# Transposes of adjacent columns, new order lists, and the first x in two loads

## The reference

```
memory_proj = ctx @ W_mem.T
attn        = softmax(x @ memory_proj.T / sqrt(256))
mem         = attn @ memory_proj
gate        = sigmoid(concat[x, mem] @ W_gate.T + b_gate)
x1          = rmsnorm(x + gate * mem) * norm_w

q           = layernorm(x1) * g + b, @ Wq / 8          # 16 heads of 64
k, v        = split(ctx @ Wkv)
out         = softmax(q k.T, masked) v @ Wo
x2          = x1 + tanh(attn_gate) * out
y           = x2 + tanh(ff_gate) * gelu(layernorm(x2) @ W1) @ W2
```

## Time and profile before

| | |
|---|---|
| median of 3 runs | 211.98 us (211.62 to 212.43) |
| profiled execution | 211.99 us |
| its span in the trace | 210.2 us |
| TensorE matmuls | 203.1 us, 97% of the span |
| TensorE weight loads | 170.2 us, 81% |
| VectorE | 152.5 us, 73% |
| ScalarE | 130.7 us, 62% |
| GpSimd | 73.0 us, 35% |

### The profile page before, as it was taken

How to read it: one execution, slowest core, us unless ns; L and a number is a source line. 1 busy time by engine, 2 the same in 40 slices (tenths; PEclk the granted TensorE clock), 3 DMA queues, 4 the chain that set the end, 5 groups by cost and what they waited for, 6 DMA issues and landing times.

```text
span 210.2 us, 4475 instructions
## 1 busy us (share of the span) xinstructions
PE 203.1 (97%) x1497; PEld 170.2 (81%) x1497; DVE 152.5 (73%) x534; ACT 130.7 (62%) x412; POOL 73.0 (35%) x69
## 2 busy tenths in 40 slices
PE   7899999999999999999999999989999999999993
PEld 3568768988778988888878988877877799988993
DVE  2499997869987788889778889999787464234410
ACT  3378687169974696583687677768997740158400
POOL 1010427633357033145333544794385006000000
PEclk9999999999999999999999999999999999999999
DMA  6996500140000000000000000006000000100011
GB/s 192 310 371 204 174 25 2 28 176 0 3 0 2 0 5 0 3 3 0 3 0 5 0 2 3 0 0 203 3 0 3 0 0 28 53 25 0 6 50 58
DMA packets 8797, 10.19 MB, mean 48 GB/s; under 512 B 1088, under 2 KB 7872, under 8 KB 8512
## 3 DMA queue, kind: packets, MB, share of 16 engines
q1 hardware_dynamic: 8096, 9.44, 13.9%
q10 hardware_dynamic: 672, 0.39, 0.6%
HBM read 8.79 MB, written 1.05 MB: 47 GB/s over the span
## 4 chain that ended last, share of the span: by engine, by line
PE 68%; DVE 9%; issue 8%; POOL 8%; DMA 4%; SPq 2%; ACT 0%; POOLq 0%; DVEq 0%
PE bank L509 44%; PE bank L1321 5%; PE bank L1293 5%; PE bank L1433 5%; DMA probs<-in_L_xattn_W_gate_dram 4%; PE bank L1331 4%; POOL probs L623 3%; SPq L556 2%; PE bank L1276 2%; DVE xhat L1033 1%; PE bank L1359 1%; DVE expd L971 1%; POOL xhat L660 1%; DVE fused L1006 1%; POOL roots L635 1%
## 5 line engine op out<-in xcount | busy, mean ns | idle before, releaser
L623 POOL TENSOR_TENSOR probs<-expd,row_rcp 128x512 f32<-128x512 f32 x39 | 41.6, 1088 | 61.3 <-DVE row_rcp L981 61.3
L751 ACT ACTIVATE expd<-expd,neg_max 128x128 f32<-128x128 f32 x128 | 49.6, 393 | 1.5 <-DVE neg_max L971 1.4
L971 DVE CUSTOM_DVE_ANT_0 expd<-bank,mask_bias 128x128 f32<-128x128 f32 x128 | 28.5, 285 | 4.5 <-PE bank L1293 3.9
L509 PE MATMUL bank<-xhT_pair,wq_pair 128*128 128x256 f32 x192 | 26.2, 290 | 0.4 <-DVE fused L1006 0.2
L509 PE MATMUL bank<-wo_pair,oT_pair 128*128 128x256 f32 x192 | 26.2, 288 | 0.0
L509 PEld LDWEIGHTS bank<-xhT_pair,wq_pair 128*128 128x128 f32 x192 | 23.9, 190 | 2.3 <-issue 1.0
L509 PEld LDWEIGHTS bank<-wo_pair,oT_pair 128*128 128x128 f32 x192 | 24.1, 191 | 1.6 <-issue 1.0
L751 ACT ACTIVATION_READ_ACCUMULATOR expd<-expd,neg_max 128x1 f32 x128 | 24.5, 192 | 0.0
L509 PE MATMUL bank<-wq_pair,gelu_pair 128*128 128x256 f32 x192 | 23.7, 284 | 0.1
L509 PEld LDWEIGHTS bank<-wq_pair,gelu_pair 128*128 128x128 f32 x192 | 23.3, 192 | 0.4 <-DVE x_sb L1154 0.3
L1321 PE MATMUL bank<-ident,probs 128*128 128x128 f32 x160 | 21.1, 275 | 0.0
(11 more groups left out here) (155 smaller groups left out, 361.6 us busy)
## 6 DMA issues: line engine op xcount, KB each, us to landing
stage<-in_L_xattn_W_dram SPq DMA_DIRECT2D x2, 1024.0 KB, 5.2
x_sb<-in_x_dram SPq DMA_DIRECT2D x4, 256.0 KB, 7.8
wkv_sb<-in_L_xattn_Wkv_dram SPq DMA_DIRECT2D x2, 512.0 KB, 5.6
stage<-in_L_xattn_Wq_dram SPq DMA_DIRECT2D x1, 1024.0 KB, 9.5
stage<-in_L_xattn_Wo_dram SPq DMA_DIRECT2D x1, 1024.0 KB, 5.5
out_dram<-x_sb SPq DMA_DIRECT2D x8, 128.0 KB, 1.9
ctx_sb<-in_ctx_dram SPq DMA_DIRECT2D x4, 192.0 KB, 6.4
probs<-in_L_xattn_W_gate_dram SPq DMA_DIRECT2D x1, 512.0 KB, 8.3
```

The source lines that it names most:

```text
L509: last = nc.tensor.matmul(bank_ap, lhs(a), rhs(c), start=start and n == 0, stop=stop and n == 2)
L623: nc.gpsimd.tensor_tensor(probs[:, r, :].rearrange("p (h k) -> p h k", h=hb), expd[:, r, :].rearrange("p (h k) -> p h k", h=hb), row_rcp[: ...
L751: last = nc.scalar.activation(here, here, ACT.Exp, bias=neg_max[:, r, h:h + 1], scale=-1.0, accum_out=row_sum[:, r, h:h + 1])
L971: last = nc.vector.tensor_tensor_reduce(expd[:, r, h * w:(h + 1) * w], SC[n % 2][:, h * w:(h + 1) * w], mask_bias[:, first:first + w], -1. ...
```

## The change

Part k now holds the adjacent columns 128k to 128k + 127: all transposes of x, gate weights and normalised rows read neighbouring columns, and the loads of `wq`, `w1`, W_mem and the two vectors of the first layer norm are laid out to match, as `(k p)`. x of batch 0 comes as two loads of 128 rows, one behind the other on SP's queue, each with its own semaphore, and its transposes go tile by tile instead of part by part. The warm-up has six matmuls instead of eight, and they read 128 columns four times over, so that only these are zeroed. All four lists are new; they hold the same stages. Lists are cut below; hunks that only repeat a shown edit are left out.

```diff
--- before.py
+++ after.py
@@ -30,7 +30,7 @@
 FAR = 3.0e38
 RMS_EPS = 1e-6
 LN_EPS = 1e-5
-WARM_UP = 8
+WARM_UP = 6
 DUMMIES = (3, 2)
@@ -42,111 +42,110 @@
 TENSOR_ORDER = (
-    ("xT", 0), ("ctxT", 0), ("tiles",), ("y", 0), ("look", "PE"), ("branch", "PE"), ("dummy", 0), ("ctxT", "hot"),
-    ("scores", "ctx", 0, 0), ("dummy", 1), ("v", "hot", 0, 0), ("v", "hot", 0, 1), ("weights",),
-    ("spread", "ctx", 0, 0), ("xT", 1), ("ctxT", 1), ("gatemem",), ("u", 0), ("k", "hot", 0), ("k", "hot", 1),
-    ("gate", 0), ("k", "hot", 2), ("k", "hot", 3), ("k", "hot", 4), ("y", 1), ("v", "hot", 1, 0),
-    ("scores", "ctx", 1, 0), ("k", "hot", 5), ("k", "hot", 6), ("v", "hot", 1, 1), ("xhT", 0), ("v", "hot", 2, 0),
-    ("xT", 2), ("k", "hot", 7), ("ctxT", 2), ("spread", "ctx", 1, 0), ("q", 0, 0), ("q", 0, 1), ("ctxT", 3),
-    ("scores", "head", 0, 0), ("u", 1), ("q", 0, 2), ("scores", "head", 0, 1), ("gate", 1),
-    ("scores", "head", 0, 2), ("q", 0, 3), ("spread", "head", 0, 0), ("v", "hot", 2, 1), ("scores", "head", 0, 3),
-    ("av", 0, 0), ("y", 2), ("v", "hot", 3, 0), ("spread", "head", 0, 1), ("xT", 3), ("scores", "ctx", 2, 0),
-    ("wo", 0, 0), ("xhT", 1), ("y", 3), ("av", 0, 1), ("spread", "head", 0, 2), ("q", 1, 0), ("q", 1, 1),
-    ("av", 0, 2), ("scores", "head", 1, 0), ("spread", "head", 0, 3), ("q", 1, 2), ("spread", "ctx", 2, 0),
...
-    ("spread", "head", 2, 1), ("q", 3, 0), ("q", 3, 1), ("spread", "head", 2, 2), ("av", 2, 1),
-    ("scores", "head", 3, 0), ("wo", 2, 0), ("q", 3, 2), ("scores", "head", 3, 1), ("av", 2, 2), ("q", 3, 3),
-    ("h2T", 0, 0), ("spread", "head", 2, 3), ("wo", 2, 1), ("scores", "head", 3, 2), ("av", 2, 3),
...
+    ("xT", 0), ("ctxT", 0), ("tiles",), ("y", 0), ("dummy", 0), ("ctxT", "hot"), ("scores", "ctx", 0, 0),
+    ("look", "PE"), ("branch", "PE"), ("v", "hot", 0, 0), ("dummy", 1), ("v", "hot", 0, 1), ("ctxT", 1),
+    ("spread", "ctx", 0, 0), ("weights",), ("u", 0), ("gatemem",), ("ctxT", 2), ("xT", 1), ("gate", 0),
+    ("k", "hot", 0), ("k", "hot", 1), ("y", 1), ("v", "hot", 1, 0), ("k", "hot", 2), ("scores", "ctx", 1, 0),
+    ("k", "hot", 3), ("k", "hot", 4), ("v", "hot", 1, 1), ("k", "hot", 5), ("xhT", 0), ("v", "hot", 2, 0),
+    ("k", "hot", 6), ("spread", "ctx", 1, 0), ("k", "hot", 7), ("xT", 2), ("v", "hot", 2, 1), ("q", 0, 0), ("u", 1),
+    ("scores", "head", 0, 0), ("q", 0, 1), ("q", 0, 2), ("scores", "head", 0, 1), ("gate", 1),
+    ("scores", "head", 0, 2), ("y", 2), ("q", 0, 3), ("spread", "head", 0, 0), ("scores", "head", 0, 3),
+    ("av", 0, 0), ("spread", "head", 0, 1), ("v", "hot", 3, 0), ("ctxT", 3), ("scores", "ctx", 2, 0), ("xhT", 1),
+    ("wo", 0, 0), ("av", 0, 1), ("spread", "head", 0, 2), ("q", 1, 0), ("q", 1, 1), ("scores", "head", 1, 0),
...
+    ("q", 2, 3), ("spread", "head", 2, 1), ("xhT", 3), ("wo", 1, 3), ("av", 2, 0), ("scores", "head", 2, 3),
+    ("q", 3, 0), ("q", 3, 1), ("spread", "head", 2, 2), ("av", 2, 1), ("scores", "head", 3, 0), ("q", 3, 2),
+    ("wo", 2, 0), ("q", 3, 3), ("spread", "head", 2, 3), ("scores", "head", 3, 1), ("av", 2, 2), ("wo", 2, 1),
+    ("scores", "head", 3, 2), ("av", 2, 3), ("spread", "head", 3, 0), ("wo", 2, 2), ("h2T", 0, 0), ("h2T", 0, 1),
...
 )
...
 SCALAR_ORDER = (
-    ("v", "hot", 0, 0), ("weights",), ("splitk",), ("spread", "ctx", 0, 0), ("xT", 1), ("splitq", 0), ("gatemem",),
-    ("u", 0), ("splitq", 1), ("k", "hot", 0), ("splitv",), ("gate", 0), ("k", "hot", 1), ("k", "hot", 2),
-    ("fuse", 0), ("k", "hot", 3), ("k", "hot", 4), ("y", 1), ("mask",), ("rms", 0), ("rms", 1), ("rms", 2),
...
     ("wmem",), ("xT", 0), ("xpair",), ("y", 0), ("branch", "ACT"), ("hotpair",), ("exp", "ctx", 0, 0),
+    ("v", "hot", 0, 0), ("splitk",), ("spread", "ctx", 0, 0), ("weights",), ("u", 0), ("gatemem",), ("splitq", 0),
+    ("xT", 1), ("splitv",), ("gate", 0), ("k", "hot", 0), ("fuse", 0), ("y", 1), ("mask",), ("v", "hot", 0, 1),
...
 )
...
 VECTOR_ORDER = (
-    ("wmem",), ("any",), ("xT", 0), ("ctxT", 0), ("flag",), ("branch", "DVE"), ("ctxT", "hot"), ("xpair",),
-    ("scores", "ctx", 0, 0), ("hotpair",), ("norm", "ctx", 0, 0), ("v", "hot", 0, 0), ("v", "hot", 0, 1),
-    ("weights",), ("spread", "ctx", 0, 0), ("splitk",), ("xT", 1), ("ctxT", 1), ("gatemem",), ("u", 0),
...
-    ("q", 3, 0), ("q", 3, 1), ("ln2", 1), ("av", 2, 1), ("scores", "head", 3, 0), ("norm", "head", 2, 3),
-    ("spread", "head", 2, 2), ("split1", 0), ("q", 3, 2), ("scores", "head", 3, 1), ("norm", "head", 3, 0),
-    ("q", 3, 3), ("x2hat", 1), ("av", 2, 2), ("norm", "head", 3, 1), ("spread", "head", 2, 3), ("split1", 1),
...
+    ("any",), ("xT", 0), ("wmem",), ("ctxT", 0), ("flag",), ("xpair",), ("branch", "DVE"), ("ctxT", "hot"),
+    ("scores", "ctx", 0, 0), ("norm", "ctx", 0, 0), ("v", "hot", 0, 0), ("v", "hot", 0, 1), ("ctxT", 1),
+    ("spread", "ctx", 0, 0), ("hotpair",), ("weights",), ("splitk",), ("u", 0), ("gatemem",), ("ctxT", 2),
...
+    ("q", 3, 0), ("ln2", 1), ("split1", 0), ("spread", "head", 2, 2), ("norm", "head", 2, 3), ("q", 3, 1),
+    ("av", 2, 1), ("scores", "head", 3, 0), ("split1", 1), ("q", 3, 2), ("spread", "head", 2, 3),
+    ("norm", "head", 3, 0), ("scores", "head", 3, 1), ("av", 2, 2), ("x2hat", 1), ("norm", "head", 3, 1),
...
 )
...
 POOL_ORDER = (
-    ("norm", "ctx", 0, 0), ("branch", "POOL"), ("splitv",), ("rms", 0), ("norm", "ctx", 1, 0), ("xhat", 0),
-    ("splito", 0), ("splito", 1), ("norm", "head", 0, 0), ("norm", "head", 0, 1), ("rms", 1),
...
+    ("norm", "ctx", 0, 0), ("branch", "POOL"), ("splitv",), ("rms", 0), ("norm", "ctx", 1, 0), ("splito", 0),
+    ("xhat", 0), ("norm", "head", 0, 0), ("splito", 1), ("norm", "head", 0, 1), ("rms", 1), ("xhat", 1),
...
 )
@@ -375,6 +374,7 @@
         x_in = [sem(f"x_in{b}") for b in range(B)]
+        x0_rest_in = sem("x0_rest_in")
         ctx_arrived = [sem("ctx_first_in"), sem("ctx_hot_in"), sem("ctx_rest_in")]
         w_in = {n: sem(f"{n}_in") for n in ("mask", "tiles", "wmem", "wgate", "bgate", "normw", "ln", "lnq", "gates", "wkey",
                                             "wvalue", "wq", "wo", "w1", "w2")}
@@ -532,7 +532,7 @@
         def mem_view(part):
-            return gate_mem_pair[:, part, D:2 * D].rearrange("e (p k) -> e k p", k=K)
+            return gate_mem_pair[:, part, D:2 * D].rearrange("e (k p) -> e k p", k=K)
         def mem_bank(bank_ap):
             return bank_ap[:, 0:D].rearrange("e (k p) -> e k p", k=K)
@@ -558,7 +558,8 @@
             def load_x(b):
                 load(x_sb[:, b * T:(b + 1) * T, :], x[b].rearrange("(t p) d -> p t d", p=P), x_in[b])
-            load_x(0)
+            load(x_sb[:, 0, :], x[0, 0:P, :], x_in[0])
+            load(x_sb[:, 1, :], x[0, P:N, :], x0_rest_in)
             load(mask_tiles[:, :], mask.rearrange("b (t n) -> (b t) n", n=P), w_in["tiles"])
             load(wkv_sb[:, INNER:2 * INNER], wkv[:, INNER:2 * INNER], w_in["wvalue"])
             load(ctx_tiles[:, 1:B, HOT, :], ctx_in[1:B, HOT * P:M, :].rearrange("b p e -> p b e"), ctx_arrived[1])
@@ -569,10 +570,11 @@
             load(wgate_sb, w_gate.rearrange("(k p) f -> p k f", p=P), w_in["wgate"])
             load_x(1)
             load(bgate_sb[:, :], b_gate.rearrange("(a d) -> a d", a=1).to_broadcast([P, D]), w_in["bgate"])
-            load(stage[:, :].rearrange("p (k n) -> p k n", k=K), wq.rearrange("(p k) n -> p k n", k=K), w_in["wq"])
+            load(stage[:, :].rearrange("p (k n) -> p k n", k=K), wq.rearrange("(k p) n -> p k n", k=K), w_in["wq"])
             load(normw_sb[:, :], norm_w.rearrange("(a d) -> a d", a=1).to_broadcast([P, D]), w_in["normw"])
-            for i, v in enumerate((lnq_g, lnq_b)):
-                load(lnq_cols[:, i, :], v.rearrange("(p k) -> p k", k=K), w_in["lnq"])
+            with nc.allow_non_contiguous_dma(reason="two values a row"):
+                for i, v in enumerate((lnq_g, lnq_b)):
+                    load(lnq_cols[:, i, :], v.rearrange("(k p) -> p k", k=K), w_in["lnq"])
             load(mask_u8[:, :], mask.rearrange("(a b) m -> a (b m)", a=1).to_broadcast([P, B * M]),
                  w_in["mask"])
             with nc.allow_non_contiguous_dma(reason="single values"):
@@ -588,7 +590,7 @@
             load(stage[:, :].rearrange("p (i n) -> p i n", n=D), wo.rearrange("(i p) n -> p i n", p=P), w_in["wo"])
             sp.wait_ge(act["wsplit"], 4)
             sp.wait_ge(pool["wsplit"], 2)
-            load(stage[:, :].rearrange("p (k n) -> p k n", k=K), w1.rearrange("(p k) n -> p k n", k=K), w_in["w1"])
+            load(stage[:, :].rearrange("p (k n) -> p k n", k=K), w1.rearrange("(k p) n -> p k n", k=K), w_in["w1"])
             sp.wait_ge(act["wsplit"], 6)
             sp.wait_ge(dve["wsplit"], 4)
             load(stage[:, :].rearrange("p (i n) -> p i n", n=D), w2.rearrange("(i p) n -> p i n", p=P), w_in["w2"])
@@ -683,7 +685,7 @@
         @block.scalar
         def _(sc):
-            sc.dma_start(wmem_sb[:, :, :], w_mem.rearrange("(p k) e -> p k e", k=K)).then_inc(w_in["wmem"], 16)
```

(27 more changed lines are left out.)

97 lines of the change are left out of this document (49 added, 48 removed), and 35 rows, old and new, of tables (SCALAR_ORDER, TENSOR_ORDER, VECTOR_ORDER).

## The result

| | before | after |
|---|---|---|
| median | 211.75 us (211.26 to 212.43, 18 runs) | 213.6 us (211.58 to 214.75, 18 runs) |
| ratio, 95% interval | | 1.0072, 1.0052 to 1.0092 |
| span of the profiled execution | 210.2 us | 212.4 us |

The changed kernel is slower by about 1.5 us at the middle of the interval; the forecast was 1.3 us faster.

The account below looks back on a forecast made before the run. TensorE's queue was taken as the bound, matmuls busy 203.1 us, 97% of the span. Start -0.1, transposes -0.5 and lists -0.7 summed to -1.3, from 211.98 to 210.7 us; range 209.4 to 212.5.

Parts of the forecast that it names:

- The lists behind 35 us: New engine orders after 35 us: 0.7 us gained, no work added; bounds from 1.2 lost to 1.6 recovered.
- the cover of `av 2 3` and of the second `xhT`: Work hiding two old waits: 5.0 us instead of 2.7 at the first, gaining 0.7; 2.3 less at the second, even.
- The gain of the lists: Behind 35 us, the new lists give back 0.7 us at the context product that had waited 0.8.
- The transposes: Adjacent columns make 52 transposes 10 ns faster each, 110 ns start to start: 0.5 us gained on TensorE.
- Rival (b): Transposes no faster with adjacent columns, by the skill's 16-byte-line rule: 211.2 us; chance 0.06.
- The start: Start to 35 us: 0.1 us gained; scores at 8.1, 0.9 earlier, the gain mostly spent from 13 to 35 us.
- x's half at 4.2: At the start, the first 128 KB half of x was taken to land at 4.2 us.
- The loads behind it 0.50 later: On SP's queue, every load behind x leaves 0.50 us later because x takes two loads.
- the hand sum of VectorE's list: VectorE's work up to `q 0 0`, put at 35.5: sum 0.15 us lost, or 0.5 gained if shorter; 0.1 gained taken.
- Rival (c): Clock stays low longer at the start, rising only behind the scores; 2.5 us lost, 213.2 us; chance 0.12.
- Rival (a): List gain doesn't come: VectorE waits at `gate 0`, `q 0 0` and second `xhT` replace those removed; 211.8 us; chance 0.27.
- The signs I listed: Trace checks: six warm-ups, scores near 8.1, 141 ns weight loads; wrong if VectorE stalls TensorE over 1 us at 35-60.

## Why the prediction was wrong

**The forecast, 210.7, was wrong in sign**, and the range of 209.4 to 212.5 did not hold the 213.6. By its own steps:

- *The lists behind 35 us* is the step that failed: the term put the cost of new waits at nothing, and a wait of 1.9 us with a fall of the clock of 1.7 us behind it stood there. I went through the holes of the old lists and asked whether each comes back; the new hole is at a place that had none. I looked at the cover of `av 2 3` and of the second `xhT`, and wrote "No work is added". Three moved entries meet at `gate 1`: `splitq 1` behind `xhT 0` (which I did weigh, but only for `q 0 0`), `splito` on ScalarE behind `u 1` with its second half on GpSimd between two normalisations, and `y 2` from behind `av 0 0` to right behind `scores head 0 2`, where it takes the bank of the first half of `gate 1` and waits for its addition. Price: 1.9 us of waiting and 1.7 us of lower clock, the latter in about half of the executions. The prediction named no bank in this step, and the SP wait for the staging buffer I had not followed to `wo`.
- The gain of the lists was right as far as it went: new lists with the hole filled against the same kernel with old lists are 0.6 (17 dummies) to 0.9 us faster (ratios 0.9961 and 0.9947 against 0.9988), where 0.7 was forecast, and the wait at `av 2 3` went from 0.8 to 0.3. By medians, each against before of its own series, it is 0.45 and 0.6. (Between `av 2 3` and its spread stand two head scores, `av 2 2` and an output product, 4.7 us of work, and no query product: a slip of 0.3 without effect.)
- *The transposes*: 141 ns loads and 109 ns from start to start, as forecast; worth 0.25 us instead of 0.5 (interval 0 to 0.5). Rival (b), that they aren't faster, is refuted at the instruction, though not by the time, whose interval reaches 0. The Trainium skill, "SBUF — State Buffer", 16-byte lines, expects no cost from every second fp32 column; the trace differs, 206 to 208 ns against 141.
- *The start* was mis-sized in sign. "x's half at 4.2": 3.25. "The loads behind it 0.50 later": issued 0.39 later for the hot context but landed 1.9 later, and this is what set the scores at 9.85 and not at 8.1. Normalisation 14.36 and not 12.9, `u 0` 16.16 and not 14.9, `gate 0` 20.05 and not 19.4, `q 0 0` 36.0 and not 35.5. That is +0.6 in equal work at `q 0 0` where I took -0.1; with the old start and new lists (ten dummies) it is 1.2 *ahead* of before there. So the hand sum of VectorE's list was too dark and the start too bright. The old lists pay 0.8 for the changed start; the new ones seem to pay more, perhaps since they put VectorE's copies on the chain from 12 to 20 us, which no run isolates.
- *Rival (c)*, the clock rises late, came true at its place: `y 0` at half pace and the rise inside the first scores, past the 8 us that I had set. Its price of 2.5 us did not: the changed kernel is 0.6 behind at `q 0 0`, and so, 0.7, is its version with 17 dummies, whose `y 0` took 1.10. In both the scores had to wait for the hot context (9.11 and 9.78). Its reason, the pauses behind six warm-ups, isn't shown either: the six other traces with six warm-ups rose in time, and the other late rise was behind eight (with a wait of 0.6 us for the first context). The sentence on transposes that don't count as activity ("TensorE: Matmul & The Clock Gate", Part 4, in the Trainium skill) fits this trace, in which four slow transposes of x and four of the context lay between warm-ups and a `y 0` at the lower level all through; other traces of the same start, with the same transposes, rose in them (0.94 for the four of x, 1.10 for `y 0`), so the runs don't settle it.
- *Rival (a)* named the right kind, a wait on VectorE in place of the removed ones, and the wrong places and price (211.8).
- The signs I listed did their work: warm-ups six, 141 ns, 109 ns, no 0.8 wait and the gate weights before 14 (13.63) held; "VectorE lets TensorE wait over 1 us between 35 and 60" named the failure, and the first scores did run in part at the lower level (2.16 against 1.88).

Adding up in executions with full clock: transposes -0.25, start +0.8, lists with their hole -0.6 to -0.9, sum about -0.2; measured 212.30 against 211.75, +0.55. With the fall, 1.9 more, 214.18. Some 0.7 are missing. A dearer start under the new lists would cover them: in equal work at `q 0 0` the changed kernel is 1.7 behind the new lists on the old start with ten dummies, and 2.4 behind its own version with one load. But other traces of the new lists on the old start stand anywhere from 1.4 ahead of before to 0.1 behind there, so this isn't shown.

Open: where these 0.7 are, why two loads of 128 KB in place of one of 256 KB halve the rate of the transfers from 4 to 7 us, where the lower clock sits in executions with old lists and six warm-ups, and what makes the clock rise late in some executions.

## What to carry to other kernels

When an order list is made anew, don't only ask whether the old holes return. For each bank or buffer taken in turn, find the new neighbour that must release it, the engine that reads it, the very instruction that raises the count (here not the last reader but the one behind it), and what GpSimd runs at that time. A hole of 2 us in the engine that bounds the kernel cost itself and, in about half of the executions here, again as much in clock. Cheap filler in it took 0.9 to 1.2 us back; only with the old start as well did the loss of 1.5 us become a gain of 1.1 (by the ratios). At the start, an earlier first tile is worth nothing when the transfers behind it set the next wait, as the hot context's landing did.

## What the runs showed of the hardware

- VectorE's addition of two SBUF operands (128x256, 0.42 us alone) waits for GpSimd's 128x1024 operation: it ended 0.27 or 0.28 us after GpSimd's in each of the ten traces where it was started beside it, and so lasted 1.71 to 1.74 us where much was left of that (eight traces), 0.63 or 0.64 where little was. With GpSimd idle it took 0.42. Its neighbour that reads a bank (L1006) kept its 0.41 to 0.42 us beside the same operation. The Trainium skill, "SBUF — State Buffer", section "SBUF: two separate sides", has this as a lock: of a VectorE operation with two SBUF inputs and a GpSimd operation that reads SBUF, the one that starts first keeps the shared ports for the whole instruction and the other "fully blocks". The traces agree, 1.72 us against 0.42; I had not looked for such a meeting when I weighed the lists.
- After a hole of 1.9 us at `y 2` the granted clock went to 0.50 and stayed there for 3.4 us, in all four traces with this hole; after 0.4 to 0.7 us there it stayed at 1.00 (three traces). It is no rule for a single hole: the 2.5 us at `wo 0 0` left the trace at 1.00, and of the two traces with over 2 us in front of the hot context (2.2 and 2.4) one fell and one did not. With the hole at `y 2`, 32 of 54 executions had the lower clock, so one profile of such a kernel shows one of two kernels.
- With two loads of x in place of one, the same bytes, the transfers moved 137 to 184 GB/s in place of 354 to 394 from 4 to 5 us (seven traces against eleven), with the DMA share at 0.88 to 1.13 against 1.05 to 1.19. Why is open.
